# A two-layer Mamba, expert and attention kernel: taps built by broadcast, 71 expert tiles, and a first scan unit in which VectorE weighs all sixteen states

## Chip, core and metric

One core of a Trainium2 chip runs the whole program in one launch. The metric is the device time of the program in microseconds; lower is better. All data are fp32.

## The reference

Two layers, each `x = x + s * silu(g)` with `s` and `g` computed from a layer norm of `x`, which is 8 batches of 512 rows of 256.

```python
# layer 0
xn = layernorm(x)
s  = mamba_forward_and_backward(xn)   # below
g  = silu(experts(xn))                # softmax router over 8 experts, best 2; 512 hidden, silu(a) * b
x  = x + s * g
# layer 1
s = memory_attention_with_three_mlp_levels(layernorm(x))
g = silu(linear(layernorm(x)) + low_rank_correction)
x = x + s * g

def branch(xz, ...):                  # one direction; 512 channels, 16 states
    x, z = split(xz)
    x = silu(conv(x, 4 taps for each channel) + bias)
    dt = softplus(...); B, C = ...    # from x
    for each of the 16 states n:
        h_n[l] = exp(dt[l] * A_n) * h_n[l-1] + dt[l] * B_n[l] * x[l]
    y = sum_n C_n[l] * h_n[l] + x * D
    return y * silu(z)
```

## The kernel before

The program has three parts. The routing block normalises all of x, picks two experts for each row and gives each row a place (`slot`) in a list of tiles of 128 rows, sorted by expert (`owner` holds each tile's expert). The scan block runs the Mamba layer and the experts beside each other. The last part runs layer 1.

**Scan block.** A batch has two units: d = 0 forward and d = 1 backward, so there are 16 units. A unit has 16 steps, one for each state n. Channels lie on partitions, in DB = 4 blocks of 128. For each state, GpSimd forms `hs = u * B` (L733, the row of B read from `bb`, broadcast), ScalarE writes the decays `dA` (L827), VectorE scans them in two halves (L927), TensorE turns the result in four chunks into PSUM (`turn`, L1058, two banks `hT`), and VectorE weighs each chunk with the state's C and adds it to `yacc` (`weigh`, L935 and L937). There are four buffers `hs`, so GpSimd can form state n only when state n - 4 has been turned or added. Two states of a unit, `POOLN = (2, 9)`, are weighed by GpSimd instead: it multiplies by a broadcast row of C (L702, the row loaded into `cb` by SP) and adds the product to `ysum` (L715). For the first of them in a forward unit the other operand is the skip term x * D, which ScalarE leaves in `xc[0]` (L835). At the end of a batch TensorE adds `ysum` and `yacc`, VectorE multiplies with the gate (`finish`) and TensorE applies the output projection.

Each engine has its own hand-written order. VectorE's step n holds the scans of state n + 2 and the four weighings of state n. In the same steps TensorE and ScalarE prepare the next unit (`PREP`: projections `proj`, L1024; convolutions `conv`, L1031; `xd`, `dt`, `c`, `gate`), at fixed half steps, all through the one PSUM bank `prep`. The softplus sums (`soft`) are GpSimd's. The backward unit of a batch reuses the projection of the forward one.

**Convolution.** The four taps are two pairs. `xpad` holds each block twice, for its two halves of channels, with the data shifted by one column between upper and lower partitions, so that one matmul of 128 rows applies two taps to 64 channels. The weights of these matmuls, `taps`, are diagonal 64x64 blocks, made once at the start of the scan block by VectorE, 64 instructions (L911). ScalarE fills `xpad` from PSUM with four copies for each block (L778, L779).

**First unit.** Nothing runs beside its preparation: TensorE, ScalarE and VectorE work through `proj`, `conv`, `xd`, `dt` and `soft` one behind another, with four PSUM banks in turn, until `u` is ready. Meanwhile GpSimd scatters the normalised rows to their places in `xg_scratch` (`group`, L684, an indirect transfer; 18 chunks of rows early, two transfers each, and one chunk behind each of the states 0 to 13 of the first unit). The scratch was filled with zeros in the routing block.

**Expert tiles.** A tile has six pieces (`x`, `a`, nothing, `b`, `gate`, `down`) in consecutive half steps, from the starts in `TILE_AT`. TPB = 10 tiles belong to a batch. The first five of a batch run in its backward unit, the other five in the forward unit of the next batch. There are 75 tiles: the last unit has five too, with starts of its own, at every fifth half step. Up to 71 can be in use.

## Time and profile before

| | us |
|---|---|
| median of 3 runs | 3221.01 (3220.27 to 3221.54) |
| the profiled execution | 3221.54 |
| its span, first to last instruction | 3219.8 |
| routing block | 0 to 84 |
| first state formed by GpSimd | 170 |
| scan block ends | 2186 |

Over the whole span TensorE is busy 82%, VectorE 70%, ScalarE 56% and GpSimd 55%. A timeline row gives the start in the span, the length, engine, line, operation, tile written and tiles read, how many instructions the row merges, and in brackets how long the engine was idle before it and what released it. PEclk is TensorE's granted clock as a share of full speed. DVE is VectorE, ACT ScalarE, POOL GpSimd, PE TensorE.

### The profile page before, as it was taken

Reading aid. Unit: us, or ns where it says so; the run is one execution under the profiler, and the core shown is the slowest. Engines: PE = TensorE matmul, PEld = TensorE weight load, DVE = VectorE, ACT = ScalarE, POOL = GpSimd, SP = SyncE. Lnnn points to the kernel's source line nnn. Section 1 sums busy time; section 2 is a strip of 40 time slices with the busy share of each in tenths; the row PEclk is TensorE's granted clock in tenths of the full one; section 3 lists DMA queues with packets and bytes.
Section 4 is the critical chain, followed back from the end, with each engine's and each line's share of the span. In section 5 each row is a group of like instructions: output and inputs, shape, how many; then the busy total and the mean of one; then the engine's idle time right before and its main releaser. Section 6 shows DMA issues by size and latency. Waiting matters only on the chain. (4 is left out here: it accounts for less than half of the span.)

```text
span 3219.8 us, 40563 instructions
## 1 busy us (share of the span) xinstructions
PE 2645.9 (82%) x13486; PEld 1749.8 (54%) x13486; DVE 2264.5 (70%) x2844; ACT 1799.5 (56%) x2771; POOL 1755.9 (55%) x554
## 2 busy tenths in 40 slices
PE   5445887878878878878878878667999999999999
PEld 5123565565565555555556556555555555555554
DVE  5368989989989989989989999984442442442430
ACT  1255868858768868858858868631332332332322
POOL 0489888878778788788788888761000000000000
PEclk9766989989989989989989989887999999999999
DMA  7213333324334333433433333323000000000000
GB/s 256 83 57 104 106 105 129 129 80 149 108 105 139 119 106 119 139 106 116 141 108 116 114 133 116 107 88 131 27 33 0 33 33 0 33 30 3 7 7 7
DMA packets 149593, 283.24 MB, mean 88 GB/s; under 512 B 23979, under 2 KB 98198, under 8 KB 149398
## 3 DMA queue, kind: packets, MB, share of 16 engines
q1 hardware_dynamic: 143254, 264.11, 23.9%
q0 software_dynamic: 6144, 16.79, 1.5%
q8 instruction: 91, 1.49, 0.2%
q14 instruction: 104, 0.85, 0.1%
HBM read 239.16 MB, written 41.68 MB: 87 GB/s over the span
## 5 line engine op out<-in xcount | busy, mean ns | idle before, releaser
L733 POOL TENSOR_TENSOR hs<-u,bb 128x2048 f32<-128x2048 f32 x256 | 1159.3, 4537 | 315.6 <-PE hT L1058 263.3
L927 DVE TENSOR_TENSOR_SCAN hs<-dA,hs 128x1024 f32<-128x1024 f32 x512 | 1166.3, 2284 | 115.6 <-POOL hs L733 91.0
L1058 PE MATMUL hT<-ident,hs 128*128 128x128 f32 x3584 | 573.6, 301 | 343.6 <-DVE held L937 300.8
L827 ACT ACTIVATE dA<-dt,cols 128x511 f32<-128x511 f32 x1024 | 661.6, 681 | 308.6 <-DVE hs L927 303.4
L1058 PEld LDWEIGHTS hT<-ident,hs 128*128 128x128 f32 x3584 | 434.5, 152 | 496.3 <-DVE held L937 372.1
L937 DVE SCALAR_TENSOR_TENSOR held<-hT,ct,held 128x512 f32<-128x512 f32 x864 | 602.2, 741 | 29.2 <-PE hT L1058 27.6
L1332 ACT ACTIVATE gl<-bank,cols_sb 128x512 f32<-128x512 f32 x192 | 130.8, 688 | 528.0 <-PE bank L1571 527.7
L1571 PE MATMUL bank<-mT,cms_sb 128*128 128x512 f32 x768 | 363.6, 598 | 10.1 <-ACT mT L1326 8.6
L137 POOL COPY cur<-slot 128x8 uint32 (+1 forms) x8 | 1.5, 188 | 639.8 <-DVE held L149 630.3
L1077 PEld LDWEIGHTS moe<-xgT,held 128*128 128x128 f32 x2400 | 307.8, 206 | 55.7 <-issue 27.5
L1077 PE MATMUL moe<-xgT,held 128*128 128x128 f32 x2400 | 321.6, 291 | 13.1 <-ACT xgT L841 12.8
L1582 PE MATMUL bank<-gl,cms_sb 128*128 128x512 f32 x512 | 242.2, 600 | 7.3 <-issue 3.8
L1571 PEld LDWEIGHTS bank<-mT,cms_sb 128*128 128x128 f32 x768 | 144.4, 191 | 164.7 <-issue 147.5
L1083 PE MATMUL moe<-held,sa 128*128 128x256 f32 x600 | 185.0, 464 | 15.6 <-DVE sa L947 15.5
L1399 DVE TENSOR_TENSOR sm<-bank,mask 128x512 f32<-128x512 f32 x128 | 82.5, 686 | 137.0 <-PE bank L1466 136.1
L1083 PEld LDWEIGHTS moe<-held,sa 128*128 128x128 f32 x600 | 140.4, 244 | 58.5 <-DVE sa L947 28.1
L1024 PE MATMUL prep<-xnT,w_in 128*128 128x512 f32 x244 | 134.6, 679 | 43.2 <-DMA xnT<-xnT_scratch 17.4
L702 POOL TENSOR_TENSOR hs<-hs,cb 128x2048 f32<-128x2048 f32 x32 | 145.4, 4543 | 31.5 <-DVE hs L927 31.5
L827 ACT ACT_TABLE_LOAD x123 | 157.8, 1283 | 3.7 <-issue 1.5
L1582 PEld LDWEIGHTS bank<-gl,cms_sb 128*128 128x128 f32 x512 | 92.9, 190 | 114.2 <-issue 101.2
L1031 PE MATMUL prep<-xpad,taps 128*64 128x512 f32 x488 | 121.7, 620 | 8.4 <-ACT xc L788 5.0
L1372 DVE TENSOR_TENSOR vp<-bank,vmask 128x256 f32<-128x256 f32 x64 | 24.2, 420 | 141.9 <-PE bank L1518 141.6
(224 smaller groups left out, 3359.6 us busy)
## 6 DMA issues: line engine op xcount, KB each, us to landing
held<-wl SPq DMA_DIRECT2D x75, 1024.0 KB
bb<-b_scratch SPq DMA_DIRECT2D x128, 512.0 KB, 5.3
held<-wl SPq DMA_DIRECT2D x75, 512.0 KB
xg_scratch<-zero SPq DMA_DIRECT2D x10, 960.0 KB, 5.4
xg<-xg_scratch SPq DMA_DIRECT2D x75, 128.0 KB
yg_scratch<-yg SPq DMA_DIRECT2D x75, 128.0 KB, 1.7
held<-x SPq DMA_DIRECT2D x16, 512.0 KB, 8.4
cb<-b_scratch SPq DMA_DIRECT2D x32, 256.0 KB, 4.8
```

What stands on the lines that cost most here:

```text
L702: nc.gpsimd.tensor_tensor(hs[m % HS][:, :, :], hs[m % HS][:, :, :], row, ALU.mult).then_inc(p_mul, 1)
L733: nc.gpsimd.tensor_tensor(hs[n % HS][:, :, :], u[d][:, :, :], row, ALU.mult).then_inc(dBu_ready, 1)
L827: last = nc.scalar.activation(dst, src, ACT.Exp, scale=cols[:, at:at + 1])
L927: nc.vector.tensor_tensor_scan(h, decay, h, 0.0, ALU.mult, ALU.add).then_inc(scan_done, 1)
L937: ins = nc.vector.scalar_tensor_tensor(out=yacc[:, c, :], in0=hT[c % 2][:, :], scalar=ct[d][:, c, n:n + 1], in1=yacc[:, c, :], op0=ALU.mul ...
L1024: last = mm(dst[:, :], w_in[:, j, at:at + P], xnT[:, j, :], start=(j == 0), stop=(j == KD - 1))
L1058: last = nc.tensor.transpose(hT[c % 2][:, k * P:(k + 1) * P], hs[n % HS][:, k, c * P:(c + 1) * P], ident[:, :])
L1077: last = mm(moe[:, m * P:(m + 1) * P], w1[r][:, k, (at + m) * P:(at + m + 1) * P], xgT[:, k, :], start=(k == 0), stop=(k == KD - 1))
L1083: mm(moe[:, 0:DM], sa[:, m, :], w2[r][:, m, :], start=(m == 0), stop=False)
L1332: nc.scalar.activation(gl[h % 2][:, :], bank[4 + h % 2][:, :], ACT.Gelu_apprx_tanh, bias=col(C1 + HM * lv + h))\
L1571: last = mm(bank[4 + h % 2][:, :], cms1_sb[:, lv, k, h * P:(h + 1) * P], mT[lv][:, k, :], start=(k == 0), stop=(k == KD - 1))
L1582: last = mm(bank[6 + k][:, :], cms2_sb[:, lv, h, k * P:(k + 1) * P], gl[h % 2][:, :], start=(h == 0), stop=(h == HM - 1))
```

## The change

- **Taps.** Eight VectorE instructions instead of 64: for each direction, half of the output channels and half of the partitions one multiplication of 64x512, the unit rows of `ident` and the tap values both broadcast.
- **xpad.** Only the edge columns are set to zero. For the first unit's projection ScalarE makes two of the four copies, VectorE the other two (64x512 out of PSUM), and each first convolution waits for both (`halves`).
- **First unit.** `by_pool` is empty for it: GpSimd weighs and adds no state there, VectorE weighs all sixteen and TensorE turns all sixteen. ScalarE writes the first unit's skip term into `ysum`, and the second unit's first addition starts from there. The counts of the semaphores (`turned`, `adds`, `cb_in`, `p_mul`, `p_add`) shift by the two that are missing. SP loads no C row for GpSimd in the first unit, except the one for the second unit, and waits for no weighing before it.
- **71 tiles.** T0 = 5 and NT = 71, so the last unit has one tile, at half step 0. The zero fill has nine transfers of up to 2048 columns instead of ten of 1920.

```diff
-T0 = (TPB + 1) // 2
-NT = TPB * NB - T0
+T0 = 5
+NT = 2 * TC + NE - 1
...
-                per = NT * DM // TPB
-                for i in range(TPB):
+                for i in range(N_ZERO):
...
-                    sp.dma_start(flat[:, i * per:(i + 1) * per], zero[:, 0:per]).then_inc(zeroed, 16)
+                    at = range(NT * DM)[i * ZERO:(i + 1) * ZERO]
+                    sp.dma_start(flat[:, at[0]:at[-1] + 1], zero[:, 0:len(at)]).then_inc(zeroed, 16)
...
             def turned(unit, n):
 
-                return NW * unit + n - sum(m < n for m in POOLN)
+                if unit_is_first(unit):
+                    return n
+                return NW * unit + NP + n - sum(m < n for m in POOLN)
+
+            def by_pool(unit):
+
+                return () if unit_is_first(unit) else POOLN
...
-                starts = range(0, 5 * T0, 5) if last and d == 1 else TILE_AT[d]
-                for i in range(TPB - T0) if d == 1 else range(-T0, 0):
+                starts = TILE_AT[d]
+                for i in range(-T0, 0) if d == 0 else range(NT - TPB * (NB - 1) if last else TPB - T0):
...
                 store_b(0, 0)
                 for p in range(2):
                     load_pair(0, p)
-                load_c(0, POOLN[0])
...
                             for k, m in enumerate(POOLN):
-                                if n == m + 2 and (k < NP - 1 or more):
-                                    sp.wait_ge(p_mul, NP * unit + k + 1)
+                                if n == m + 2 and (k < NP - 1 or more) and (k == NP - 1 or not unit_is_first(unit)):
+                                    if not unit_is_first(unit):
+                                        sp.wait_ge(p_mul, NP * (unit - 1) + k + 1)
                                     load_c(d if k < NP - 1 else 1 - d, POOLN[(k + 1) % NP])
...
                             state(d, unit, b, n)
-                            for k, m in enumerate(POOLN):
+                            for k, m in enumerate(by_pool(unit)):
...
                     if what == "proj":
-                        for g in range(2):
+                        for g in range(1 if first else 2):
...
-                    nc.scalar.activation(xc[d][:, k, :], xc[d][:, k, :], ACT.Copy, scale=cols[:, at:at + 1]).then_inc(skip_ready, 1)
+                    dst = ysum if unit_is_first(unit) else xc[d]
+                    nc.scalar.activation(dst[:, k, :], xc[d][:, k, :], ACT.Copy, scale=cols[:, at:at + 1]).then_inc(skip_ready, 1)
...
                 for g in range(2):
-                    nc.vector.memset(xpad[g][:, :, :], 0.0).then_inc(hT_used, 1)
+                    nc.vector.memset(xpad[g][:, :, 0:KC - 1], 0.0).then_inc(edges, 1)
+                    nc.vector.memset(xpad[g][:, :, KC - 2 + L:], 0.0).then_inc(edges, 1)
...
                 for d in range(2):
-                    for k in range(DB):
-                        for g in range(2):
-                            for q in range(KC // 2):
-                                for half in range(2):
-                                    rows_ = slice(HP * half, HP * (half + 1))
-                                    at = (d * DB + k) * KC + tap_of(d, q, int(half != g))
-                                    nc.vector.tensor_scalar(taps[rows_, d, k, g, q, :], ident[rows_, rows_], w_tap[rows_, g, at:at + 1],
-                                                            None, ALU.mult).then_inc(taps_ready, 1)
+                    for g in range(2):
+                        for half in range(2):
+                            own = slice(HP * half, HP * (half + 1))
+                            tap = w_tap[own, g, DB * KC * d:DB * KC * (d + 1)].rearrange("p (k q t a) -> p k q t a", q=KC // 2, t=2, a=1)
+                            whole = [HP, DB, KC // 2, HP]
+                            unit_rows = ident[own, own].rearrange("p (a b c) -> p a b c", a=1, b=1).broadcast_to(whole)
+                            nc.vector.tensor_tensor(taps[own, d, :, g, :, :], unit_rows,
+                                                    tap[:, :, :, tap_of(d, 0, int(half != g)), :].broadcast_to(whole),
+                                                    ALU.mult).then_inc(taps_ready, 1)
...
+                dve.wait_ge(edges, 4)
+                for k in range(DB):
+                    use = use_of("proj", k, 0, 0)
+                    dve.wait_ge(p_ps, use + 1)
+                    nc.vector.tensor_copy(xpad[1][HP:P, k, KC - 1:KC - 1 + L], home(use, True)[HP:P, :])
+                    nc.vector.tensor_copy(xpad[1][0:HP, k, KC - 2:KC - 2 + L], home(use, True)[HP:P, :]).then_inc(halves, 1)
                 for quarter in range(4):
                     soft(dve, 0, 0, quarter)
...
                         if first and k == 0:
-                            pe.wait_ge(taps_ready, 4 * DB * KC)
+                            pe.wait_ge(taps_ready, 8)
+                        if first:
+                            pe.wait_ge(halves, k + 1)
...
-                                for c in (2 * j, 2 * j + 1) if n not in POOLN else ():
+                                for c in (2 * j, 2 * j + 1) if n not in by_pool(unit) else ():
```

## Rows read from the trace of the kernel before

**Rows 1.** Windows, one stretch of a middle unit; columns: stretch, us, busy by engine, PEclk, DMA.
```profile
340.00:460.00 120.00, 95.43 (x524) 71.13 (x523) 108.68 (x107) 84.75 (x135) 99.56 (x25) 0.90 0.35 117
```

**Rows 2.** Timeline of VectorE (DVE) at the start: start, us, instruction, [idle before].
```profile
77.03 0.78 DVE L326 TENSOR_TENSOR own<-ends,iota_t 128x600 f32<-128x600 f32 x1
...
89.12 1.78 DVE L902 MEMSET xpad<- 128x2072 f32 x1 [0.38 <-issue]
90.82 20.35 DVE L911 TENSOR_SCALAR taps<-ident,w_tap 64x64 f32<-64x64 f32 x64
```

**Rows 3.** Instructions that write the tile taps: shortest, median and longest, in ns.
```profile
L911 DVE TENSOR_SCALAR taps<-ident,w_tap x64: 125/251/450, 90.8 to 110.9; 64x64 f32<-64x64 f32 x64
```

**Rows 4.** Timeline of TensorE (PE) at the start.
```profile
111.32 3.68 PE L1031 MATMUL hT<-xpad,taps 128*64 128x512 f32 x8 [17.45 <-issue]
...
117.75 1.94 PE L1031 MATMUL prep<-xpad,taps 128*64 128x512 f32 x8
119.62 1.98 PE L1024 MATMUL moe<-xnT,w_in 128*128 128x512 f32 x4
...
138.24 3.68 PE L1031 MATMUL hT<-xpad,taps 128*64 128x512 f32 x8 [14.77 <-ACT xpad L779]
```

**Rows 5.** Timeline of ScalarE (ACT) at the start.
```profile
135.05 0.69 ACT L788 ACTIVATE xc<-prep,cols 128x512 f32<-128x512 f32 x1 [14.38 <-remote]
```

**Rows 6.** Timeline of GpSimd (POOL), from the start to the second unit.
```profile
130.10 0.97 POOL L684 DMA_INDIRECT xg_scratch<-held,slot  x1 [0.30 <-issue]
169.99 4.50 POOL L733 TENSOR_TENSOR hs<-u,bb 128x2048 f32<-128x2048 f32 x1 [38.91 <-DVE u L557]
...
304.13 9.01 POOL L733 TENSOR_TENSOR hs<-u,bb 128x2048 f32<-128x2048 f32 x2
```

**Rows 7.** Groups of GpSimd's instructions, 169 to 304 us: busy us, mean ns, idle before.
```profile
L733 POOL TENSOR_TENSOR hs<-u,bb 128x2048 f32<-128x2048 f32 x16 | 72.4, 4527 | 39.2 <-DVE u L557 38.9
L684 POOL DMA_INDIRECT xg_scratch<-held,slot x28 | 27.7, 988 | 6.6 <-issue 6.4 <-POOL ysum L715 0.2
```

**Rows 8.** Timeline of VectorE in the first unit.
```profile
188.60 4.47 DVE L927 TENSOR_TENSOR_SCAN hs<-dA,hs 128x1024 f32<-128x1024 f32 x2 [2.54 <-POOL hs L733]
...
196.45 2.28 DVE L927 TENSOR_TENSOR_SCAN hs<-dA,hs 128x1024 f32<-128x1024 f32 x1
...
247.42 2.28 DVE L927 TENSOR_TENSOR_SCAN hs<-dA,hs 128x1024 f32<-128x1024 f32 x1
...
254.41 2.29 DVE L927 TENSOR_TENSOR_SCAN hs<-dA,hs 128x1024 f32<-128x1024 f32 x1
...
308.76 2.29 DVE L927 TENSOR_TENSOR_SCAN hs<-dA,hs 128x1024 f32<-128x1024 f32 x1 [1.90 <-POOL hs L733]
```

**Rows 9.** Timeline of TensorE in the first unit.
```profile
232.07 1.94 PE L1058 MATMUL hT<-ident,hs 128*128 128x128 f32 x8 [1.62 <-DVE held L937]
...
264.26 3.78 PE L1024 MATMUL prep<-xnT,w_in 128*128 128x512 f32 x4 [2.06 <-ACT ct L799]
```

**Rows 10.** Windows, a stretch of the first unit.
```profile
204.00:304.00 100.00, 58.97 (x222) 32.46 (x219) 76.65 (x62) 59.93 (x83) 95.05 (x39) 0.74 0.21 70
```

**Rows 11.** Timeline of VectorE in the last unit and behind it.
```profile
2102.71 1.10 DVE L947 SCALAR_TENSOR_TENSOR sa<-moe,b,sa 128x128 f32<-128x128 f32 x4
...
2133.84 2.29 DVE L927 TENSOR_TENSOR_SCAN hs<-dA,hs 128x1024 f32<-128x1024 f32 x1 [2.99 <-POOL hs L733]
...
2196.90 0.68 DVE L1373 COPY kv<-bank 128x512 f32<-128x512 f32 x1
```

**Rows 12.** Waits of VectorE, 2045 to 2165 us: us in total, times, longest.
```profile
DVE held L937 <- PE hT L1058: 5.8, 5, 2.7
DVE hs L927 <- ACT dA L827: 3.0, 2, 1.9
```

**Rows 13.** Timeline of GpSimd in the last unit.
```profile
2106.58 4.52 POOL L733 TENSOR_TENSOR hs<-u,bb 128x2048 f32<-128x2048 f32 x1 [4.08 <-PE hT L1058]
```

**Rows 14.** Windows, the close of the scan block.
```profile
2165.00:2180.00 15.00, 13.50 (x71) 10.68 (x69) 11.37 (x24) 2.94 (x3) 0.00 (x0) 1.00 0.21 70
```

More of the change, by code:

```diff
@@ L216, in bass_mamba_moe_then_linear_attention_mlp @@
         EARLY = 18
+        ZERO = 2048
+        N_ZERO = -(-NT * DM // ZERO)
         layR = ExitStack()
@@ L224, in bass_mamba_moe_then_linear_attention_mlp @@
             xaT = [sr(f"xaT{i}", [P, KD, L]) for i in range(2)]
-            zero = sr("zero", [P, 2048])
+            zero = sr("zero", [P, ZERO])
             w_r = sr("w_r", [P, KD, NE])
@@ L474, in bass_mamba_moe_then_linear_attention_mlp @@
             setup_v, setup_g, setup_a, taps_ready = sem("setup_v"), sem("setup_g"), sem("setup_a"), sem("taps_ready")
-            xnT_in, p_ps, p_used = sem("xnT_in"), sem("prep_ps"), sem("prep_used")
+            xnT_in, p_ps, p_used, edges, halves = (sem(n) for n in ("xnT_in", "prep_ps", "prep_used", "xpad_edges", "first_halves"))
             xc_ready = sem("xc_ready")
@@ L564, in tile_pieces @@
                 out = {s: [] for s in range(2 * NS)}
-                starts = range(0, 5 * T0, 5) if last and d == 1 else TILE_AT[d]
-                for i in range(TPB - T0) if d == 1 else range(-T0, 0):
+                starts = TILE_AT[d]
+                for i in range(-T0, 0) if d == 0 else range(NT - TPB * (NB - 1) if last else TPB - T0):
                     for at, piece in enumerate(("x", "a", "", "b", "gate", "down")):
-                        out[starts[i % T0] + at].append((piece, i))
+                        out[starts[i + T0 if d == 0 else i] + at].append((piece, i))
                 return out
@@ L652, in body @@
                                     sp.dma_start(yg_dram[bass.ds(t * P, P), :], yg[i % RING][:, :]).then_inc(y_st[i % RING], 16)
-                                    if not (last and i + RING >= TPB - T0):
+                                    if not last or TPB * (NB - 1) + i + RING < NT:
                                         load_tile(t + RING, i)
@@ L705, in add @@
                     m = POOLN[k]
-                    pool.wait_ge(p_mul, NP * unit + k + 1)
+                    pool.wait_ge(p_mul, NP * (unit - 1) + k + 1)
                     other = ysum
@@ L712, in add @@
                             pool.wait_ge(o_ps, 2 * b)
+                    elif k == 0 and unit_is_first(unit - 1):
+                        pool.wait_ge(skip_ready, DB)
                     else:
@@ L725, in state @@
                         pool.wait_ge(bb_in[n // 2 % 2], 16 * (4 * unit + n // 4 + 1))
-                    if n >= HS and n - HS in POOLN:
+                    if n >= HS and n - HS in by_pool(unit):
                         pool.wait_ge(p_add, adds(d, b, POOLN.index(n - HS)) + 1)
@@ L761, in _ @@
                 act.sem_inc(yg_ready, 1)
-                act.wait_ge(hT_used, 2)
+                act.wait_ge(edges, 4)
                 def output(b, h, src):
@@ L786, in prepare @@
                         if k == 0 and not (isinstance(unit, int) and unit < 2):
-                            act.wait_ge(p_add, N_ADD * b + (NP if d == 0 else 0))
+                            if d == 1:
+                                act.wait_ge(p_add, N_ADD * b - NP)
+                            elif later(b):
+                                act.wait_ge(p_add, N_ADD * b)
                         nc.scalar.activation(xc[d][:, k, :], src[:, :], ACT.Identity,
```

18 lines of the change are left out of this document (10 added, 8 removed).

## The prediction

> **What bounds the kernel now.** I read the table of windows first, to see which engine fills each stage, then the timelines of the start, of the first unit and of the last unit. In the middle of the program the sixteen scan units are VectorE's: it is busy 108.7 of 120 us [rows 1]. What makes one unit shorter there moves all that follows, for nothing in those units waits for a clock of its own. Three places are different, and the change touches all three. At the start of the scan block VectorE builds the tap matrices for 20.35 us [rows 2] while TensorE sits idle for 17.45 us before the first convolution [rows 4]; later ScalarE waits 14.38 us for convolution 1 [rows 5], and only when the first unit's u is ready, at 169.99 us, can GpSimd form the first state [rows 6]. In the first unit GpSimd is the bound: from 169.99 to 304.13 it has no pause [rows 6], since it also issues 28 scatter transfers and weighs and adds two states [rows 7], and the scan that opens the second unit comes at 308.76 us, straight behind a GpSimd state [rows 8]. In the last unit there is no next unit to prepare, and VectorE waits for TensorE, for ScalarE and for GpSimd [rows 12]. The last third (attention and MLP) is TensorE's and nothing in the diff touches it; it moves with what lies ahead.
>
> **The start.** VectorE's path to the first convolution: the two memsets of xpad at 1.78 us each [rows 2] become four of 9 to 12 columns. I take 0.25 us for one, the median of the small tap instructions [rows 3], so 3.6 us become 1.0: 2.6 earlier, taps begin at 90.8 - 2.6 = 88.2. Sixty-four instructions (20.35 us [rows 2]) become eight of 64x512. The nearest row of a two-operand instruction with a broadcast operand is 128x600 at 0.78 us [rows 2]; I take that for each, 6.2 us, ending at 94.4. Its bounds: 0.25 us each (2 us), or for two strange strides at once three times as long (19 us, and the edit gives only the memsets back). Then 0.2 us for the negated decay columns, and VectorE's own new work, the two half copies out of PSUM for channel block 0. A copy 128x512 out of PSUM took 0.68 us [rows 11], so 1.4 us: convolution 0 can start at 96.0 instead of 111.32 [rows 4]: **15.3 us earlier**. The other three pairs of copies (4.1 us) fall where VectorE has nothing else; ScalarE makes two copies instead of four for each block meanwhile, which I count at nothing.
>
> The second item of the start is the wait of 14.38 us. The row is odd: convolution 1's matmuls were issued from 117.75 on, ahead of the projection at 119.62 [rows 4], yet ScalarE was released at 135.05, by something that the profile cannot name [rows 5]. In those us GpSimd issued scatter after scatter, the last at 130.10 [rows 6]. The change does not speak of this wait. It does move the whole chain of projection and convolutions to some 95 to 112 us, ahead of 119, and it takes 56 of VectorE's 64 signals away. I take it as gone: **14.4 us**, with both ends kept: nothing of it gained, or all. The rest of the chain (silu, the x projection, dt, softplus) is unchanged. The first state moves from 169.99 to 140.3, which is behind GpSimd's last early scatter (130.10 [rows 6]), so the scatters do not hold it. TensorE's clock is an uncertainty of some us: eight convolution matmuls took 3.68 us at 111.32 and 1.94 at 117.75, four projection matmuls 1.98 us at 119.62 and 3.78 at 264.26 [rows 4, 9], a ratio of 1.9, the two levels of 1.2 and 2.4 GHz. Four convolutions and three projections could cost or give 5 us.
>
> A rule is weighed here against a row. The tap instructions overlapped GpSimd's scatter issues of 0.97 us [rows 6] and none took more than 0.45 us [rows 3], so no tap instruction waited out a whole issue. The Trainium skill, SBUF — State Buffer, section "SBUF: two separate sides", says that a VectorE instruction with two SBUF inputs and a GpSimd instruction that reads SBUF lock a shared port pair for their whole length, and the new taps have two SBUF inputs where the old had one. By the row the sum is as above; by the rule, see the rivals.
>
> **The first unit.** Removed from GpSimd: two weighings and two additions of 128x2048, each taken at the 4.53 us of a state of that size [rows 7]: 4 x 4.53 = 18.1 us off a chain without pause. What GpSimd still does: from the first state to the first state of unit 1, 134.1 - 18.1 = 116.0 us. Added to VectorE: eight weighings. A step with two scans and four weighings takes 6.99 us (247.42 to 254.41 [rows 8]). GpSimd's step with a state and two scatter issues is 4.5 + 2 x 1.0 and gaps of 0.25 + 0.3 us, 7.0 us: 72.4 + 27.7 + 6.4 over the unit [rows 7]. So the two engines now run at one pace. VectorE's step 0 began 18.6 us behind the first state, at 188.60, and step 1 7.9 us later, at 196.45 [rows 8]; step 14, which holds the first scan of unit 1, would start at 18.6 + 7.9 + 13 x 6.99 = 117.4 us behind the first state if VectorE never waits; GpSimd's state for it is done at 116.0 + 4.5 = 120.5. GpSimd stays the bound by 3.1 us, and step 14 starts at 120.5 instead of 308.76 - 169.99 = 138.8 us behind the first state [rows 6, 8]: 18.3 us at most.
>
> What eats of that: TensorE must now turn all sixteen states. Four chunks of a state are 2 x 1.94 us at 232.07 [rows 9], at 1.2 GHz, and the clock in this unit was 0.74 of full speed, TensorE busy 59 of 100 us [rows 10]. Steps with two convolutions or two gate projections for unit 1 ask 3.9 + 2 x 3.7 = 11.3 us of TensorE at 1.2 GHz against VectorE's 6.99: up to 4.3 us late, and there are two such steps (3 and 10). Until now GpSimd's pauses hid them. 3.1 us of slack take some; I count 2 us of loss: **16 us gained**, bounds 12 and 18.3. Behind GpSimd's chain, SP's queue: the first load of the C row for GpSimd goes, the load for unit 1 at step 11 no longer waits for a weighing, and the tiles' loads at step 14 wait for scatters that are now issued earlier by the same 16 to 18 us; all of it stays as far ahead of its user as before. The skip term goes to ysum instead of xc, the same ScalarE instruction.
>
> **71 tiles.** Nine zero transfers instead of ten, 5% fewer bytes, at a time when VectorE's routing chain ends the stage: nothing. The four tiles that go were always the last four of the last unit. Their cost on VectorE: in steps 4 and 7 one gate each (four instructions, 1.1 us, 1.0 in the chain [rows 11]), of the 3.0 us of waits for ScalarE the longer, 1.9, and of the 5.8 us in five waits for TensorE [rows 12] a third, 1.9, as an estimate: tile 0 keeps its part of the longest, 2.7, and one in step 7 and those behind it lie where GpSimd sets the pace. That is 5.9 us by the time GpSimd starts state 11 at 2106.58 [rows 13]. From there six GpSimd instructions of 4.5 us lead to the scan at 2133.84, with 3.0 us of waiting on VectorE ahead of it [rows 11]: what is saved in steps 8 to 10 is swallowed by that chain. The gate of step 12 gives 1.0 more: **7 us**. Bounds: 8.5 us, if all waits for TensorE go, and 0 if the thinner work lets TensorE's clock fall where it closes the scan block: there it was at full clock and busy 13.5 of 15 us [rows 14]; were half of that at 1.2 GHz, some 7 us would be lost.
>
> **Sum.** The profiled execution took 3221.54 us (span 3219.8, 1.7 us around it), the median is 3221.01. 15.3 + 14.4 + 16 + 7 = 52.7: 3221.5 - 52.7 = **3169 us**.
>
> **The rivals.**
> - *The odd wait stays.* It keeps its length, or it is bound to the scatters and ends when they end. For: it ended 4 us behind the last scatter issue [rows 5, 6], which the change does not move. If it keeps its 14.4 us, the start gives 15.3: 3183. If it holds TensorE's signals until 135 wherever the chain is by then, the chain has come further and the start gives something between 15.3 and 29.7; I take 19: 3180.
> - *The odd wait swallows the start whole*: convolution 1 is answered at 135 whatever went before. Then only the first and the last unit give: 3221.5 - 23 = 3198. Against it: the chain will be through all four convolutions before the time at which signals were late at all.
> - *Taps wait for GpSimd.* Each of the eight waits out one issue of 0.97 us: 7.8 us less, 3177. The rule of the skill named above would do this; the row of tap durations is against it.
> - *TensorE jams the first unit*: all the steps where states are turned, not only two, cost 11.3 us. 13 x 4.3 = 56 us, less 3 of slack, against 18.3 won: unit 0 would be 35 us longer, and with a start that gives 15.3 and a last unit that gives 7 the kernel is slower, 3221.5 + 35 - 22 = 3234. It decides from a mean step of 6.99 + (18.3 + 3.1 + 22) / 13 = 10.3 us. Against it: TensorE has 59 us of work in 100 [rows 10]; eight more chunks are 16 us.
> - *It does nothing*: that would need start, first unit and last unit all hidden. The units behind are VectorE's with no fixed time, so I see no cover.
>
> On the odd wait a page bears too: the Trainium skill, VectorE: DVE Perf Modes, section on the TRN2 errata, warns that dense signals on completion from one engine can block another's. No run here shows that it was this. By it, with 56 signals gone, the wait would go, which is the forecast's 3169; without it, 3180 to 3183.
>
> **Numbers.** Forecast (3169, own range 3160 to 3177) 0.45; the wait stays (3180 to 3183) 0.28; it swallows the start (3198) 0.10; taps wait (3177) 0.03; a first unit that gives only part, with either start (3173 to 3190) 0.10; the jam 0.03; a startup better than forecast (full clock, cheap taps: down to 3157) 0.01. The range from 3156 to 3191 leaves out the swallowed start, the jam and some of the edges, about 2 in 10. A measurement of this kernel can tell about 0.2%, 6.4 us, from no change. Faster by more than that 0.95, within it 0.02, slower 0.03.
>
> **What would show it.** First state on GpSimd near 140 us (step right), near 151 to 155 (wait stays), near 170 (swallowed). Tap instructions: eight of under 0.8 us. From the first state to unit 1's first scan 120 to 123 us; VectorE in that stretch with waits for TensorE of 2 to 6 us and GpSimd without pause. From step 0 of the last unit to the end of the scan block 7 us less. The prediction is wrong if the wait's place turns out to have nothing to do with what moved, if the tap instructions are slow, or if units 1 to 14 change length.

## The result, and the profile after

The changed kernel takes a median of 3173.0 us (3168.24 to 3178.19, 4 runs) against 3221.28 us (3220.27 to 3221.82, 4 runs) for the kernel before: a ratio of 0.9846, with a 95% interval of 0.9833 to 0.9859. Forecast were 3169 us, with a range of 3156 to 3191. The profiled execution took 3172.15 us, its span is 3170.4 us: 49.4 us less than before.

The timeline of VectorE at the start (rows as in [rows 2]; the last row is a half copy for channel block 2, VectorE's new work):

```profile
86.52 0.07 DVE L918 MEMSET xpad<- 128x12 f32 x1
...
86.53 0.66 DVE L930 TENSOR_TENSOR taps<-ident,w_tap 64x512 f32<-64x512 f32 x1
...
87.22 5.00 DVE L930 TENSOR_TENSOR taps<-ident,w_tap 64x512 f32<-64x512 f32 x7
...
97.94 0.69 DVE L1004 COPY xpad<-hT 64x512 f32<-64x512 f32 x1 [2.60 <-issue]
```

The memsets of the edges take 0.07 us each and the first tap instruction starts beside them, at 86.53. Eight tap instructions take 5.7 us where 64 took 20.35 [rows 2]. The timeline of TensorE over the same stretch:

```profile
94.06 1.94 PE L1060 MATMUL hT<-xpad,taps 128*64 128x512 f32 x8 [0.37 <-DVE xpad L1005]
...
101.62 3.65 PE L1060 MATMUL hT<-xpad,taps 128*64 128x512 f32 x16
112.44 5.62 PE L1065 MATMUL prep<-xc,w_x 128*128 128x512 f32 x8 [7.16 <-ACT xc L807]
121.00 1.13 PE L1070 MATMUL moe<-xdT,w_dt 128*128 128x512 f32 x2 [2.94 <-issue]
...
122.82 0.60 PE L1068 MATMUL hT<-ident,xdT 128*128 128x128 f32 x4
```

Convolution 0 begins at 94.06 instead of 111.32 [rows 4]: 17.3 us earlier. From there the gain shrinks and grows again by turns. The timeline of ScalarE, which answers to [rows 5]:

```profile
104.07 0.69 ACT L803 ACTIVATE xc<-hT,cols 128x512 f32<-128x512 f32 x1 [1.15 <-PE hT L1060]
108.38 0.69 ACT L803 ACTIVATE xc<-hT,cols 128x512 f32<-128x512 f32 x1 [3.63 <-remote]
...
120.35 0.60 ACT L811 ACTIVATE xdT<-prep 128x512 f32<-128x512 f32 x1 [8.06 <-remote]
125.25 0.69 ACT L820 ACTIVATE dt<-moe,cols 128x512 f32<-128x512 f32 x1 [4.30 <-PE prep L1070]
...
136.45 0.22 ACT L814 ACTIVATE ct<-hT 128x64 f32<-128x64 f32 x1 [3.67 <-remote]
```

"Remote" is a release that the profile cannot name. The single wait of 14.38 us [rows 5] has become several. Read each against TensorE's rows above: the last convolution's matmuls end at 105.3, ScalarE is released at 108.38; the x projection ends at 118.1, the release is at 120.35; the transposes of xdT end at 123.4, the release is at 136.45, 13 us later (ScalarE had other work until 132.8, so only 3.67 of them are idle time). The row at 125.25 is a late one as well: TensorE's product for it ended at 122.1, and the releaser that the row names belongs to another tile. GpSimd's timeline shows what goes on beside them, and when the first state comes:

```profile
85.13 1.17 POOL L694 DMA_INDIRECT xg_scratch<-held,slot  x1 [0.71 <-issue]
86.61 1.44 POOL L694 DMA_INDIRECT xg_scratch<-held,slot  x1 [0.31 <-issue]
...
130.99 0.97 POOL L694 DMA_INDIRECT xg_scratch<-held,slot  x1 [0.30 <-issue]
147.54 4.50 POOL L745 TENSOR_TENSOR hs<-u,bb 128x2048 f32<-128x2048 f32 x1 [15.58 <-DVE u L567]
```

The first state is 22.5 us earlier than at 169.99 [rows 6]. The four issues that lie beside the new taps take 1.12 to 1.44 us instead of 0.97 or 0.98, so the burst ends 0.9 us later than before (its last issue was at 130.10 [rows 6]). The first unit, in VectorE's timeline (the scan that opens unit 1, as in [rows 8]) and in its waits from 147 to 269 us (us in total, times, longest; most of the 12.0 are the waits for the first three states, in which nothing else is ready, and 1.89 that for the last):

```profile
268.42 2.29 DVE L947 TENSOR_TENSOR_SCAN hs<-dA,hs 128x1024 f32<-128x1024 f32 x1 [1.89 <-POOL hs L745]
```

```profile
DVE hs L947 <- POOL hs L745: 12.0, 5, 4.7
DVE held L955 <- PE hT L1087: 0.6, 1, 0.6
DVE held L957 <- PE hT L1087: 0.4, 1, 0.4
DVE hs L947 <- ACT dA L842: 0.4, 1, 0.4
```

From the first state to that scan are 268.42 - 147.54 = 120.9 us, before 308.76 - 169.99 = 138.8 [rows 6, 8]. TensorE turns all sixteen states now and VectorE waits for it for 1.0 us. The window of 100 us that begins about as far behind the first state as that of [rows 10]:

```profile
181.00:281.00 100.00, 68.91 (x291) 41.79 (x290) 96.87 (x83) 65.66 (x92) 92.02 (x39) 0.76 0.31 106
```

TensorE is busy 69 of 100 us where it was 59, at a granted clock of 0.76 (it was 0.74 [rows 10]); VectorE went from 77 to 97, GpSimd from 95 to 92 [rows 10]. The last unit, VectorE's timeline and its waits from 2007 to 2119 us:

```profile
2008.16 2.27 DVE L947 TENSOR_TENSOR_SCAN hs<-dA,hs 128x1024 f32<-128x1024 f32 x1
...
2089.75 2.29 DVE L947 TENSOR_TENSOR_SCAN hs<-dA,hs 128x1024 f32<-128x1024 f32 x1 [6.51 <-POOL hs L745]
...
2115.42 3.10 DVE L957 SCALAR_TENSOR_TENSOR held<-hT,ct,held 128x512 f32<-128x512 f32 x4 [0.42 <-PE hT L1087]
```

```profile
DVE hs L947 <- POOL hs L745: 6.7, 2, 6.5
DVE held L957 <- PE hT L1087: 3.1, 4, 1.7
```

The waits for ScalarE (3.0 us [rows 12]) are gone, those for TensorE fell from 5.8 to 3.1 us [rows 12], and the wait for GpSimd's chain grew from 2.99 [rows 11] to 6.51 us: it swallows what the steps ahead of it save. Step 0 to the last weighing takes 2118.5 - 2008.2 = 110.4 us, before 2164.0 - 2045.8 = 118.2.

Where the 49.4 us of the span come from, by five points that stand in both timelines of VectorE and GpSimd:

| stretch | gain, us |
|---|---|
| start to the first state | 22.5 |
| first state to the first scan of unit 1 | 17.9 |
| from there to step 0 of the last unit | -2.7 |
| last unit, to its last weighing | 7.9 |
| from there to the end | 3.9 |

### The profile page after: what moved, and what is told of

It is laid out like the page before. It is cut to its first block and busy times, and to the rows that moved or that the text cites. A ratio compares the mean times of both kernels' runs of the same rounds, so it can differ in the third digit from the quotient of the medians.

```text
span 3170.4 us, 40091 instructions
## 1 busy us (share of the span) xinstructions
PE 2612.1 (82%) x13342; PEld 1723.8 (54%) x13342; DVE 2253.1 (71%) x2790; ACT 1776.4 (56%) x2731; POOL 1738.3 (55%) x550
## 5 line engine op out<-in xcount | busy, mean ns | idle before, releaser
L1087 PE MATMUL hT<-ident,hs 128*128 128x128 f32 x3616 | 586.3, 304 | 362.2 <-DVE held L957 312.1
L1087 PEld LDWEIGHTS hT<-ident,hs 128*128 128x128 f32 x3616 | 443.5, 154 | 521.8 <-DVE held L957 370.5
L1106 PEld LDWEIGHTS moe<-xgT,held 128*128 128x128 f32 x2272 | 289.0, 205 | 54.3 <-issue 26.4
L1106 PE MATMUL moe<-xgT,held 128*128 128x128 f32 x2272 | 302.9, 290 | 13.0 <-ACT xgT L857 13.0
L1112 PE MATMUL moe<-held,sa 128*128 128x256 f32 x568 | 173.8, 461 | 10.2 <-DVE sa L967 10.0
L1112 PEld LDWEIGHTS moe<-held,sa 128*128 128x128 f32 x568 | 131.2, 241 | 50.6 <-DVE sa L967 22.3
L712 POOL TENSOR_TENSOR hs<-hs,cb 128x2048 f32<-128x2048 f32 x30 | 136.3, 4544 | 32.4 <-DVE hs L947 32.4
```

The source lines that it names most:

```text
L712: nc.gpsimd.tensor_tensor(hs[m % HS][:, :, :], hs[m % HS][:, :, :], row, ALU.mult).then_inc(p_mul, 1)
L1087: last = nc.tensor.transpose(hT[c % 2][:, k * P:(k + 1) * P], hs[n % HS][:, k, c * P:(c + 1) * P], ident[:, :])
L1106: last = mm(moe[:, m * P:(m + 1) * P], w1[r][:, k, (at + m) * P:(at + m + 1) * P], xgT[:, k, :], start=(k == 0), stop=(k == KD - 1))
L1112: mm(moe[:, 0:DM], sa[:, m, :], w2[r][:, m, :], start=(m == 0), stop=False)
```

## The experiments

Each was timed beside runs of the kernel before in its own session; what is compared is that pair. "First state" is the start of GpSimd's first `hs = u * B` (169.99 us before [rows 6]).

**The three parts one by one.** The start's edits alone (four small memsets, eight tap instructions, ScalarE's two halves to VectorE):

```diff
-for g in range(2): nc.vector.memset(xpad[g][:, :, :], 0.0)
+for g in range(2): nc.vector.memset(xpad[g][:, :, 0:KC - 1], 0.0); nc.vector.memset(xpad[g][:, :, KC - 2 + L:], 0.0)
...
-    nc.vector.tensor_scalar(taps[rows_, d, k, g, q, :], ident[rows_, rows_], w_tap[rows_, g, at:at + 1], None, ALU.mult)
+    nc.vector.tensor_tensor(taps of d, g, half: 64x512, ident broadcast, w_tap broadcast, ALU.mult)
...
-                        for g in range(2):
+                        for g in range(1 if first else 2):
...                                            # VectorE's copies, the counts that TensorE waits for
```

> The kernel before with the start edits alone (eight broadcast tap instructions, edges of xpad, VectorE makes half of the first copies). The full change moved the first state of GpSimd from 169.99 to 147.54 us, 22.5 us. If the start's gain is carried through undiminished by the 15 units behind it, this kernel takes 3221.3 - 22.5 = 3199 us, with its first state near 147. Rival: what is gained at the start depends on late signals, which differ from run to run; then its runs spread over 5 us or more, as those of the full change did (3168 to 3178), and the mean lies anywhere from 3190 to 3206. Rival that the start is given back later: 3215 or more.

3198.23 us (3197.3 to 3203.72) against 3221.15: 0.9929 (0.9906 to 0.9953). First state at 145.36; 138.8 us from there to unit 1's first scan, as before. ScalarE's timeline has late releases here too:

```profile
107.42 0.69 ACT L788 ACTIVATE xc<-hT,cols 128x512 f32<-128x512 f32 x1 [3.23 <-remote]
...
129.89 0.23 ACT L799 ACTIVATE ct<-hT 128x64 f32<-128x64 f32 x1 [5.49 <-remote]
...
134.09 0.69 ACT L805 ACTIVATE dt<-prep,cols 128x512 f32<-128x512 f32 x1 [3.98 <-remote]
```

So it is the start's own edits, not the rest of the change, that turn one long wait into some shorter ones.

The first unit alone:

```diff
-for k, m in enumerate(POOLN):
+for k, m in enumerate(by_pool(unit)):         # () in the first unit
...                                            # counts, skip term and C rows as in the change
```

> The kernel before with the first-unit edit alone. The full change's stretch from the first state to the first scan of unit 1 went from 138.8 to 120.9 us. If that edit alone does it and the rest passes it on: first state at 170, first scan of unit 1 at 291, 3221.3 - 17.9 = 3203 us, and a spread as small as before's (under 2 us), since the start is untouched. If TensorE's turns in the first unit only fit because the start had raised its clock, the stretch is longer than 125 us and the time above 3208.

3205.06 us (3203.0 to 3209.37), 0.9946 (0.9928 to 0.9965). First state at 169.97, the wait of 13.7 us still there, unit 1's first scan at 290.80, 120.8 us behind the first state: 18.0 us gained with neither the start nor the last unit touched.

The 71 tiles alone:

```diff
-T0 = (TPB + 1) // 2
-NT = TPB * NB - T0
+T0 = 5
+NT = 2 * TC + NE - 1
...                                            # zero fill and loads for 71 tiles
```

> The kernel before with 71 tiles alone (and nine zero transfers). From the trace of the full change the last unit is 7.9 us shorter: 3213 us. The full change also showed layer 1 3.9 us shorter, although nothing in it was edited: if the four tiles are the reason (for instance transfers out of the way of layer 1's first loads, or TensorE's clock at the passage), this kernel takes 3209 to 3210; if that was TensorE's clock by chance, 3213. If GpSimd's chain swallows all of it: 3219.

3208.8 us (3205.87 to 3210.31), 0.9957 (0.9937 to 0.9976). Up to the last batch it runs 1 to 3 us behind the kernel before; the scan block ends 6.9 us earlier, and another 4.3 are gained behind it. The parts nearly add up: 3221.15 less the three medians gives 22.9 + 16.1 + 12.4 = 51.4 us, the whole change gives 48.3. Of the 12.4, the 4.3 behind the scan block need not come from the tiles: with the start alone, which keeps all 75 tiles, the last part is as short (see the stretches that are not in the sum, below).

**What makes the releases late.** The kernel before without the 36 early scatters:

```diff
-for c in range(TC - EARLY, TC):
-    group(c, grouped[0])
...                                            # and the two waits for their ends
```

It leaves out the placing of 18 of the 32 chunks of rows.

> The kernel before without the 36 early scatter transfers of GpSimd (18 of 32 chunks of rows are not placed, so the experts work on zeros there; all other work is the same). Theory that the 14.4 us wait of ScalarE for convolution 1 comes from GpSimd's scatters: the wait is gone, the first state comes at 155 to 156 us instead of 170, the time is 3207 us. Rival that it comes from VectorE's 64 dense signals, or from neither: ScalarE still waits 10 us or more between 119 and 135, and the time stays at 3221.

3203.95 us (3203.7 to 3205.64), 0.9941 (0.9919 to 0.9963). ScalarE's timeline where the wait of 14.38 us was [rows 5], TensorE's convolution 1 that it waited for, and VectorE's taps:

```profile
117.97 0.69 ACT L785 ACTIVATE xc<-prep,cols 128x512 f32<-128x512 f32 x1
```

```profile
115.43 1.94 PE L1027 MATMUL prep<-xpad,taps 128*64 128x512 f32 x8
```

```profile
91.00 17.97 DVE L908 TENSOR_SCALAR taps<-ident,w_tap 64x64 f32<-64x64 f32 x64
```

The wait is gone, and the first state comes at 151.22. The taps are 2.4 us quicker without scatters beside them, so convolution 1 stands 2.3 us earlier than at 117.75 [rows 4]; nothing else ahead of the wait has moved.

The same in the changed kernel (same work left out):

> The changed kernel without the 36 early scatters (18 of 32 chunks of rows are not placed). Theory: the four late signals between 105 and 137 us (3.6 + 8.1 + about 3 + 3.7, some 14 to 17 us) go; first state 130 to 134 instead of 147.5, time 3155 to 3161. Rival (what the profile shows as late there is TensorE itself at its lower clock or missing records): the first state stays at 145 or later and the time within 3 us of 3173.

3156.8 us (3149.53 to 3158.62), 0.9801 (0.9777 to 0.9825). First state at 132.81, 14.7 us ahead of the changed kernel's, with every wait of ScalarE for TensorE named; 3156.8 against 3173.0 is 16 us, across two sessions whose kernels before took 3220.85 and 3221.28. This row of ScalarE stands for them:

```profile
114.83 0.60 ACT L808 ACTIVATE xdT<-prep 128x512 f32<-128x512 f32 x1 [5.55 <-PE prep L1061]
```

Is it the bytes? The kernel before with narrow scatters (a quarter of each row, into an array of their own; the rest of those rows is left out):

```diff
-out=xg_dram, ..., in_=xa[:, c, :]
+out=narrow, ...,  in_=xa[:, c, 0:64]
```

> The kernel before; each of the 36 early scatters carries a quarter of its bytes (64 of 256 columns, into a scratch array of their own; the other columns of those rows are left out). Theory a (the issuing on GpSimd is what makes TensorE's signals late): 36 issues of 0.97 us as before, the odd wait stays at 12 to 15 us, first state 168 to 170, 3219 to 3221. Theory b (the bytes that the scatters move do it): the wait shrinks to a few us, first state 151 to 158, 3204 to 3209.

3221.3 us (3215.47 to 3225.56) against 3220.85, 1.0006 (0.9996 to 1.0016); first state at 169.94:

```profile
134.99 0.69 ACT L789 ACTIVATE xc<-prep,cols 128x512 f32<-128x512 f32 x1 [13.69 <-remote]
```

Not the bytes: as many transfers at a quarter of the size hold the signal nearly as long (13.69 us, where it was 14.38), until the same 135 us.

Is it VectorE's 64 signals? The kernel before, where only every eighth tap instruction signals:

```diff
-nc.vector.tensor_scalar(taps[...], ...).then_inc(taps_ready, 1)
+last = nc.vector.tensor_scalar(taps[...], ...)      # and once for eight: last.then_inc(taps_ready, 1)
```

> The kernel before with its 64 tap instructions, of which only every eighth signals its end (8 signals instead of 64). Theory (the late signals of TensorE come with GpSimd's scatter issues): nothing changes, convolution 1 is answered at about 135 us, first state at 169 to 170.5, time 3221. Rival (dense signals of VectorE are what delays it, the skill's rule on the TRN2 errata in VectorE: DVE Perf Modes): the wait of 14 us goes, first state near 156, time near 3207.

3221.73 us (3211.55 to 3227.66), 1.0 (0.9986 to 1.0014), first state at 169.59:

```profile
135.23 0.69 ACT L788 ACTIVATE xc<-prep,cols 128x512 f32<-128x512 f32 x1 [13.70 <-remote]
```

The rule of the Trainium skill that was weighed (VectorE: DVE Perf Modes, the section on the TRN2 errata) does not explain this wait: with 8 signals instead of 64 it is 13.70 us. The page itself speaks of increments at a high rate that can deadlock another engine, not of a delay.

Is it GpSimd's being busy at all? Two tries with other work in place of the scatters (which are left out again), and neither could answer, for a reason of its own:

```diff
...                                            # each with a signal, and a wait for an earlier one
+for c in range(36): nc.gpsimd.tensor_tensor(hs[3][:, c % 4, :], hs[2][:, 0, :], hs[2][:, 0, :], ALU.mult)   # kernel before
+for c in range(36): nc.gpsimd.memset(hs[2 + c % 2][...two blocks...], 1.0)                                  # changed kernel
```

> The kernel before without the 36 early scatters (the 18 chunks of rows they place are left out); in their stead GpSimd runs 36 multiplications of 128x512 of some 1.1 us, each with a signal, over the same stretch of 84 to 130 us. Theory a1 (GpSimd's being busy with anything, or its signals, makes TensorE's signals late): the odd wait stays, first state near 170. Theory a2 (only the indirect transfers, their issuing and their descriptors, do it): no such wait, first state near 151 as without scatters, time 3204.

> The changed kernel without the 36 early scatters (18 chunks of rows are not placed); in their stead GpSimd runs 36 memsets of 128x1024 of some 0.95 us, each with a signal, from 84 to about 120 us, so that the convolutions and x projection (94 to 115 us) lie beside a busy GpSimd, which they did not in the run with 36 multiplications. Theory (only the indirect transfers delay TensorE's signals): no late signal, first state at 132 to 135, time 3155 to 3160 as without scatters. Rival (any busy GpSimd with a signal for each instruction delays them): waits of 2 to 8 us behind convolution 3 and the x projection as in the changed kernel, first state at 138 to 148, time 3163 to 3173.

The first took 3224.65 us (3218.84 to 3227.46) against 3220.85, 1.0014 (1.0004 to 1.0023), first state 172.20, as if nothing had been won. But its taps, in VectorE's timeline and in the view of the tile (shortest, median, longest in ns), beside GpSimd's burst:

```profile
90.81 39.48 DVE L916 TENSOR_SCALAR taps<-ident,w_tap 64x64 f32<-64x64 f32 x64
```

```profile
L916 DVE TENSOR_SCALAR taps<-ident,w_tap x64: 237/255/973, 90.8 to 130.0; 64x64 f32<-64x64 f32 x64
```

```profile
84.97 35.93 POOL L695 TENSOR_TENSOR hs<-hs 128x512 f32<-128x512 f32 x36
```

While GpSimd multiplies (until 120.9) a tap instruction takes up to 0.97 us, the length of one GpSimd multiplication (35.93 / 36 = 1.0), and only behind that its usual 0.25. The taps end at 130.3 instead of 111.2, and the whole chain of convolutions lies behind the burst, where no signal was late. The second, in a session where the kernel before took 3197.17, took 3179.96 us (3175.64 to 3183.64), 0.9941 (0.9924 to 0.9957):

```profile
87.24 5.00 DVE L933 TENSOR_TENSOR taps<-ident,w_tap 64x512 f32<-64x512 f32 x7
92.27 24.41 DVE L938 TENSOR_SCALAR cols<-cols 128x128 f32<-128x128 f32 x1
```

The two-input tap instructions pass the memsets at 0.7 us each, but the small one-input instruction behind them (0.23 us elsewhere) is held until the 36th memset ends, at 116.6, and with it the half copies and convolution 0 (118.25). Again the chain missed the burst. And this was the session of the head start below, in which not even 32 scatters delayed a release, so the absence of a late release there would have said nothing. The changed kernel's own trace helps further. From the first state to the last weighing (148 to 2115 us) GpSimd computes nearly all the time, 92 of 100 us in the window of the first unit above, and no wait of any engine ends in a "remote" release; in the first unit, where two scatter issues stand behind each of 14 states, VectorE's waits for TensorE are 1.0 us in all. So neither computing on GpSimd nor issues in pairs between computing do it there; a burst of issues one behind the other does. What the two runs show is another thing, which is taken up at the end.

**A head start for the scatters.** As soon as the places are known (77 us) GpSimd could issue, while VectorE still works out the shares:

```diff
 # end of the routing block, GpSimd
+pool.wait_ge(placed, 1)
+pool.wait_ge(zeroed, 16 * N_ZERO)
+for c in range(TC - EARLY, TC - EARLY + 2):
+    group(c, grouped[0])
```

> The changed kernel with the first 4 of the 36 early scatters issued at the end of the routing block (from 77 us, as soon as the places are known, while VectorE still works out the shares), so that 32 are left at the start of the scan block. Theory (the signals held at the end come some 3 us behind the last scatter's transfer): the last issue at 125 to 127 instead of 131, the held signals at 130 to 132 instead of 136.4, first state at 141 to 144, time 3167 to 3170 against 3173. Rival (signals are late by the count of scatters already issued, or by the chain's own timing): first state at 146 to 149 and 3172 to 3174.

3154.95 us (3153.84 to 3156.95, 4 runs), but beside a kernel before of 3197.17 (3193.48 to 3202.71, 7 runs), not 3221: 0.9866 (0.9849 to 0.9882), less of a gain than the change without it had. No release was late, although 32 scatters ran from 85.6 us on beside the chain:

```profile
116.36 0.60 ACT L814 ACTIVATE xdT<-prep 128x512 f32<-128x512 f32 x1 [6.45 <-PE prep L1068]
```

The first state came at 134.18, where the kernel without early scatters has it (132.81). Either the head start had cured the signals, or the signals are not delayed at all where the kernel before takes 3197, and then the kernel before has no 14 us wait on it either, which would account for 17 of the 24 us that it is shorter (the run without scatters gained 17.2; the other 7 stay open). Two more runs, side by side in another session, were made to tell these apart.

> The changed kernel unaltered, to see what the machine does to it: in the session of the head start the kernel before took 3197 instead of 3221, and the head-start kernel had no late signal. Theory c (whether TensorE's signals come late beside the scatters depends on the machine or session): where the kernel before takes 3195 to 3199, the changed one takes 3153 to 3158 with its first state at 132 to 135 and no wait without a named releaser; where before takes 3221, it takes 3173 with the first state near 147.5. Theory d (the head start took the late signals away): where before takes 3197, the changed kernel still shows late signals, a first state at 145 or later and 3165 or more.

> The changed kernel with 4 of the 36 early scatters issued at the end of the routing block, once more, beside the changed kernel itself. Theory c: where before takes 3197, it equals the changed kernel within 2 us (first state about 1 us later, since the routing block ends 0.7 us later); where before takes 3221, the burst ends 4 to 5 us earlier and it takes 3166 to 3171 against 3173. Theory d: it is 10 to 18 us ahead of the changed kernel on any machine.

Here the kernel before took 3220.03 (3215.97 to 3226.11). The changed kernel took 3170.46 (3163.12 to 3173.06), 0.984 (0.9819 to 0.986), with its late releases:

```profile
107.57 0.69 ACT L803 ACTIVATE xc<-hT,cols 128x512 f32<-128x512 f32 x1 [3.19 <-remote]
...
129.38 0.22 ACT L814 ACTIVATE ct<-hT 128x64 f32<-128x64 f32 x1 [4.68 <-remote]
133.59 0.69 ACT L820 ACTIVATE dt<-prep,cols 128x512 f32<-128x512 f32 x1 [3.98 <-remote]
136.39 0.69 ACT L820 ACTIVATE dt<-moe,cols 128x512 f32<-128x512 f32 x1 [0.88 <-remote]
```

With the head start it took 3165.32 (3164.47 to 3166.23), 0.9828 (0.9812 to 0.9844), 5.1 us less than without by the medians. The intervals of the two ratios overlap, and one of the four runs without took 3163.12, so the time alone does not prove a gain; the traces do show one at the start. One release is still late:

```profile
130.11 0.69 ACT L823 ACTIVATE dt<-prep,cols 128x512 f32<-128x512 f32 x1 [3.98 <-remote]
```

Its last issue is at 126.13 us instead of 131.09, and its first state at 141.09, where the changed kernel beside it has 145.57. So the burst ends 5.0 us earlier and the first state comes 4.5 us earlier, and the delay is not cured: what was absent in the session of 3197 was the delay itself.

## Why the prediction was right, and where it was not

**The start, 15.3 us: right in kind, 2 us too small.** Convolution 0 came 17.3 us earlier. The memsets, the taps and the halves did what was worked out. The term that was off most is the memsets: with 0.25 us for each, taken from a tap instruction, the taps were to begin at 88.2; the memsets take 0.07 us and the taps begin at 86.53, 1.7 us earlier. The tap instruction, taken at 0.78 us from a row of 128x600, measured 0.66 to 0.69, which gives 0.5 us for the eight. The upper bound of 19 us for the taps had no row behind it. The rival in which taps wait out GpSimd's issues is excluded by the same rows: eight of 0.7 us, one behind the other without a pause, lie beside issues of 1.1 to 1.4 us. The rule of the Trainium skill that stood behind that rival (SBUF — State Buffer, section "SBUF: two separate sides") concerns GpSimd instructions that read SBUF; the rows say that the issue of an indirect transfer does not hold up a VectorE instruction with two SBUF inputs for its length.

**The odd wait, 14.4 us: this is the step that failed.** "I take it as gone" was wrong. It was bound to the scatters, as the first rival had it. The prediction's two reasons for it both fell: the chain had moved ahead of 119 us, but a release was late at 108.38 already, and taking VectorE's signals away changed nothing. The runs without scatters show what the wait hangs on (no early scatters, no late release, in either kernel; 17 and 16 us of time), and the runs with narrow scatters and with few signals exclude the bytes and VectorE's signals. By what path the transfers delay it stays open. In the kernel before, the chain met the delay at one point and stood until the burst was over. In the changed kernel it meets it at several, with the last signals held until 136.45 as the first one was until 135.05 [rows 5], 4 to 5 us behind the end of the last issue in both. Because the chain has come further by then, 22.5 us reach the first state instead of the forecast's 29.7: 17.3 from the edits and some 5 from the wait. The rival had put this at 19 of 29.7; the measurement lies between it and the forecast, nearer to the rival. First state on GpSimd "near 140 us (step right), near 151 to 155 (wait stays)": it was 147.5, and without scatters 132.8.

**The first unit, 16 us: right, 2 us too small.** The forecast counted 18.3 at most and took off 2 for TensorE. It gave 17.9 (18.0 alone): TensorE's extra turns were hidden nearly whole, the waits for it are 1.0 us in all. The steps feared at 11.3 us of TensorE at the lower clock were hardly seen so: of the convolutions there only the first, at 182.4 us, took 3.0 us; the three from 188.7 on took 1.94 each and the turns between them 1.2 to 1.3, at a granted clock of 1.00 (188 to 198 us), the 2.4 GHz level. TensorE had been busy 8.4 of the 10 us from 180 on. In the kernel before, the first two convolutions of this unit took 3.68 us each, at 201 and 211 us, in a window with a clock of 0.61. GpSimd remained the bound by a hair; the last state is waited for, 1.89 us [as in rows 8], and step and state run at one pace. The rival of the jam is excluded.

**The 71 tiles, 7 us: right.** Measured 7.9 in the last unit. The waits fell as told, and GpSimd's chain swallowed part of it as told: 6.51 us at the scan where 2.99 stood.

**Not in the sum.** From the first scan of unit 1 to the end of the scan block the changed kernel gives back 2.7 us, and the stretches behind give 3.9. The parts run alone do the same (start alone: 24.6 at the first state, 19.5 at the scan block's end, 24.3 at the program's end). The prediction named a changed length of units 1 to 14 as a sign of being wrong, so this has to be weighed against what kernels show that are not altered there. Six runs have the middle units and the last unit of the kernel before. From unit 1's first scan to the closing products of the scan block (VectorE's first `ysum` of the last batch) they need 1857 us (before), 1855 (narrow scatters), 1857 (few signals), 1856 (multiplications in place of scatters), and 1862 both with the start alone and without scatters. The changed kernel needs 1852 in one session and 1855 in another, with 7.9 us less in the last unit, so 1860 and 1862 on the same terms: inside that spread. From VectorE's first `vp` of layer 1 to the end the same six need 1019 (start alone) to 1026 us, and the changed kernel 1021 and 1019. So neither the 2.7 us nor the 3.9 can be laid to the change. What makes such stretches differ is not settled. In the last part TensorE's granted clock differs between windows of the same work, as this one of the changed kernel, at 0.95, where the kernel before had 0.87 from 2255 to 2290 us:

```profile
2209.00:2244.00 35.00, 34.57 (x88) 15.93 (x89) 18.75 (x48) 15.91 (x21) 7.80 (x9) 0.95 0.19 61
```

That the clock's phases are the whole of it was not tried. The profiled execution lay 3 us above the forecast: 7.2 us less at the first state were partly met by 1.9 + 0.9 + 3.9 - 2.7 us elsewhere, 52.7 - 7.2 + 4.0 = 49.5.

## What to carry to other kernels

An idle time that the profile cannot name is a term of its own: before counting it as won, ask what else runs while it lasts, and take that away in a run. Here a kernel without the transfers showed that the wait was bound to them, and the change hardly moves the time at which they end. When an engine's chain is the bound with no pause (GpSimd in the first unit), taking whole instructions off it gives their full price until the next engine's pace is reached; compare both paces before costing. And a burst of issues that others suffer from is best begun where its data is first ready: with four issues moved some 7 us forward the first state came 4.5 us earlier. Last, a stretch that the change does not touch has a spread of its own, here 7 us in 1860; before a few us there are explained, look at several kernels that are alike in it.

## What the runs showed of the hardware

- **TensorE's signals come late while GpSimd issues a burst of indirect transfers.** Up to 14.4 us in the kernel before and 13 us in the changed one, ending 4 to 5 us behind the last issue of a burst of 36; first seen at the convolution that ends at 105.3 us in the changed kernel, some 20 us into the burst, and at the one that ends at 119.7 in the kernel before, where a release at 118.26, 33 us into the burst, was still on time; with a quarter of the bytes it is as long within 0.7 us. Pairs of issues between GpSimd's computing delay nothing (28 in the first unit, waits for TensorE 1.0 us in all). ScalarE is not what is slow: in the trace of the kernel before, TensorE's increments of the semaphore that ScalarE waits for are recorded at 118.2 and then, three of them, at 135.0, 135.8 and 135.9 us, though the work behind convolution 1 had begun at 119.62 and 121.53. Whether it is the signal or TensorE's own end that is late, the traces do not tell. Records of signals also go missing beside the burst: of the 64 increments of the tap instructions the trace of the kernel before has 31 in their stretch, that of the run without scatters all 64. Every execution on record has its granted clock, so none shows whether the delay is there when nothing is recorded.
- **It is not in every session.** In four sessions of five the kernel before took 3220 to 3221 us; in one it took 3197, and a kernel with 32 scatters beside the chain had no late release there. The four sessions whose chip is on record had four different ones, so chip and session cannot be told apart. That the kernel before has none there either is inferred from its time; its trace there was not taken. A gain measured in the one kind of session is not that in the other. None of these runs says what differs.
- **One-input VectorE instructions wait for GpSimd's computing, for one of its instructions or for a whole row of them.** 64x64 products of 0.25 us took 0.97 beside multiplications of 1.0, and a 128x128 one 24.41 us instead of 0.23 beside a row of memsets without pause; two-input products of 64x512 beside the same memsets kept their 0.7 us. The Trainium skill, SBUF — State Buffer, section "SBUF: two separate sides", states this: an exclusive lock on a shared port pair, taken by VectorE's faster modes against any GpSimd instruction, by two SBUF inputs only against one that reads SBUF. The rows agree with it on which pairs collide. On the length the memset row goes further: the instruction did not wait out one memset of 0.9 us but all that were left, 24 us. Scatter issues act far more mildly: 64 taps took 20.35 us [rows 2] beside them and 17.97 without, and the issues themselves took up to 1.44 us instead of 0.97 beside the new taps.
